# Moving the weight-cast copies out of the first attention chunk, six per weight load instead of four, and loading the output projection's weights earlier

## The chip, the cores and the metric

One Trainium2 chip, all 8 cores, one launch. Every core runs the same program on its own part of the data, and no core waits for another. The metric is the device time of the slowest core in microseconds (us).

## The reference

```python
x  = hidden_states                      # (4, 2048, 2048) f32
xn = layernorm(x)
q, k, v = xn @ Wq.T + bq, xn @ Wk.T + bk, xn @ Wv.T + bv   # 16, 8, 8 heads of 128
q, k = rope(q), rope(k)                 # k, v then repeated to 16 heads
feat = lambda t: [sin(p), cos(p)] / sqrt(128),  p = (t / |t|) @ R.T
s  = ((feat(q) . feat(k_j)) weighted sum over the heads j of v_j, per token) @ Wo.T + bo
h  = silu(xn @ W1.T) * (xn @ W3.T)      # 8192 wide
g  = silu(fwht(h) @ W2.T)               # fwht: Hadamard transform of length 8192
out = x + s * g
```

The mixing of heads is per token, so nothing is carried along the sequence.

## The kernel before

A pair of cores shares one of the four batches. Each core does the attention part for all 2048 tokens of its batch and 8 of the 16 query heads, and the feed-forward part (FFN) for its own 1024 tokens.

**Attention.** `for ac in range(n_ac)` runs over 4 chunks of 512 tokens (here chunk 0 to chunk 3), each of 4 tiles of 128 tokens (`ts`). A chunk has these steps:

- `emit_ln_chunk`: SyncE loads a tile of x (`XBa`, `XBb`, L200); ScalarE takes the sum of squares by a Square whose elementwise output nobody reads (L211, into a scratch region that the argument `sqf` names); VectorE makes the mean and the normalized tile `XNa`/`XNb` (L242); TensorE transposes it, and ScalarE copies it to `XNT` (L265). The loads of the first two tiles of a chunk are issued as soon as the buffers are free, which is in the chunk before.
- QKV: six jobs (`ji` 0 to 5: two for q, two for k, two for v), each with one weight load of 2 MB of bf16, cast from 4 MB of f32 as it is loaded, alternately into `WA` and `WB`. `emit_p1g` issues the load on GpSimd's DMA queue (L335), once the job that used the buffer last is done. `emit_p1t` is the job's matmuls (L355, L359); it then has the load of job `ji + 2` issued. The last job stands apart in `emit_p1_tail` (L414, L417). For a chunk after the first, its jobs 0 and 1 have their loads issued when jobs 4 and 5 of the chunk before are done.
- features: rope on VectorE, transposes, the product with `RT16`, then for each tile `p2wrap`, `p2sin`, `p3a` (64 small products on VectorE, L721), and the mixing of values, half of it on VectorE (`p3m`, L591 to L603) and half on GpSimd (`p3p`, L739 to L749). TensorE transposes the result (L615), ScalarE copies it to `MIXT` (L625).

The chunks overlap: behind tile `ts` of the feature loop of chunk c stands job `ts + 1` of chunk c + 1, and the LayerNorm and job 0 of chunk c + 1 stand ahead of that loop. All engines take their instructions in the order of the program. On GpSimd the loads of weights and `p3p` are in one stream: `p3p` of tile 0 stands behind the load of job 3, and that waits for job 1.

**The casts.** The FFN reads its weights W1, W3 and W2 as bf16 from device memory. `emit_casts` makes these copies: 96 DMAs from device memory to device memory (L323), each reading 2 MB of f32 and writing 1 MB of bf16. They stand in `cast_list` in the order W1, W3, W2. `emit_p1g` issues 4 of them behind each of the 24 weight loads of the attention part, on the same queue:

```python
    def emit_casts(g, kmax=4):
        for _ in range(kmax):
            if cast_ptr[0] >= len(cast_list):
                return
```

Nothing in the attention part reads them; the first FFN load waits for them (`dwe`, L945).

**Output projection.** `attn_done` collects the last work of VectorE, ScalarE and GpSimd; then four blocks of 512 columns (`dc`), each with a weight load from `WOT` (`p4g`, L799) and 8 x 16 matmuls (L816). The first two loads are issued behind the last `p3p`.

**FFN.** Two passes of 512 tokens (`oc2`): LayerNorm as above from `XOWN`; W1 and W3 (L970, L975), the Hadamard transform over device memory (`S1`, `S2`), W2 (L1179), silu (L1194), the product with s and the sum with x on VectorE (L1211, L1215), and the output (L1227). The buffers of a pass's LayerNorm lie where those of the pass before for x and the output lay (`XRES`, `OUTB`), so the load at L200 waits for the output's DMAs (`out_slot_tok`).

Of the kernel before, what the change touches and what calls it, by code (L numbers as in the profile page):

```python
# [17 lines left out]
DM = 2048  # L18
# [42 lines left out]
def build_program(t_own=TOWN, t_batch=TBATCH, t_chunk=512, debug=False):  # L61
# [126 lines left out]
    def emit_ln_chunk(blk, xsrc, row0, pT, pT_free, sqf, extra_war=()):  # L188
        XBa, XBb = bufs["XBa"], bufs["XBb"]
        XNa, XNb = bufs["XNa"], bufs["XNb"]  # L190
        for ts in range(NT):
# [5 lines left out]
            def p0ld(sp, ts=ts, xb=xb, dxs=dxs):  # L197
                tk.wait(sp, "sp", *out_slot_tok, tk.tok("dbg"), *extra_war)
                tk.wait(sp, "sp", xb_cons_dv[ts % 2], xb_cons_ac[ts % 2])
                tk.inc(sp.dma_start(  # L200
                    xb[:, :],
                    bass.AP(xsrc, (row0 + ts * 128) * DM, [[DM, 128], [1, DM]]),
                ), dxs, 16)
                st["x"] = tk.tok(dxs)
# [3 lines left out]
            def p0a(a, ts=ts, xsl=xsl):  # L208
                tk.wait(a, ACT, st["x"], cst_tok, *extra_war)
                tk.wait(a, ACT, xb_cons_dv[ts % 2], xb_cons_ac[ts % 2])  # L210
                st["sq"] = tk.inc(a.activation(sqf(ts), xsl, AF.Square,  # L211
                                               accum_out=rcol(ts, C_SUMSQ)), "ac")
# [78 lines left out]
    SQF_OFF = 6144  # L291
    MIX_OFF = 10240
    sqf_attn = lambda ts: bass.AP(SBf, SQF_OFF + (ts % 2) * DM, [[SBW, 128], [1, DM]])
# [13 lines left out]

    jobs = ([(WQTS, BQs, QB, oc) for oc in range(2)]
# [8 lines left out]
    def emit_casts(g, kmax=4):  # L317
# [10 lines left out]
    def emit_p1g(blk, c, ji):  # L328
# [4 lines left out]
        def p1g(g, buf=buf, sem=sem, wd=wd, oc=oc, ji=ji, evt=evt):  # L333
# [6 lines left out]
            emit_casts(g)  # L340
# [96 lines left out]
    for ac in range(n_ac):  # L437
        arow0 = ac * t_chunk

        if ac == 0:  # L440
            with BLK() as blk:
                emit_ln_chunk(blk, XBAT, 0, [pT[0]], pT_free, sqf_attn)
                emit_p1_main(blk, 0, full=True)
                emit_p1_tail(blk, 0, None)
# [127 lines left out]
        if ac + 1 < n_ac:  # L572
            with BLK() as blk:
                emit_ln_chunk(blk, XBAT, (ac + 1) * t_chunk, [pT[0]], pT_free, sqf_attn)
                emit_p1_main(blk, ac + 1)
# [54 lines left out]
        with BLK() as blk:  # L630
            for ts in range(NT):
# [97 lines left out]
                if nxt is not None:  # L729
                    emit_p1t(blk, nxt, ts + 1)  # L730

# [58 lines left out]
    with BLK() as blk:  # L790
        evt = {}
        bank_tok = {}
        for dc in range(4):
            buf, sem = (WA, "dwa") if dc % 2 == 0 else (WB, "dwb")

            def p4g(g, dc=dc, buf=buf, sem=sem):
                tk.wait(g, "pl", tk.tok("dbg"))
                tk.wait(g, "pl", wcons[sem])
                tk.inc(g.dma_start(  # L799
                    bass.AP(buf, 0, [[8192, 128], [1, 8192]]),  # L800
                    bass.AP(WOT, dc * 128 * 8192, [[8192, 128], [1, 8192]]),
                ), sem, 16)
                evt[("w", dc)] = tk.tok(sem)
            blk.gpsimd(p4g)

            for r in range(NSUB):
                def p4t(t, dc=dc, r=r, buf=buf):
                    tk.wait(t, "pe", evt[("w", dc)], bank_tok.get(r % 4), *attn_done)
# [10 lines left out]
                    evt[("mm", dc, r)] = tk.inc(last, "pe")  # L819
                blk.tensor(p4t)  # L820

                if r % 2 == 0:
                    def p4v(v, dc=dc, r=r):
                        tk.wait(v, DVE, evt[("mm", dc, r)])
# [5 lines left out]
                else:  # L830
                    def p4a(a, dc=dc, r=r):
                        tk.wait(a, ACT, evt[("mm", dc, r)])
# [24 lines left out]
    sqf_ffn = lambda ts: bass.AP(GT8, (ts % 2) * DM, [[NT * 2 * 512, 128], [1, DM]])  # L857
# [3 lines left out]
    ffn_prev = []  # L861
    s1_free = [()]
    s2_free = [()]

    for oc2 in range(n_oc):
# [11 lines left out]
        with BLK() as blk:  # L877
            emit_ln_chunk(blk, XOWN, orow0, pT, pT_free, sqf_ffn,
                          extra_war=tuple(p4b_done) + tuple(ffn_prev))
# [55 lines left out]
        with BLK() as blk:  # L935
            upt = {}
            for gb in range(32):
# [3 lines left out]
                def p5g(g, gb=gb, b1=b1, s1_=s1_, b3=b3, s3_=s3_):  # L941
                    tk.wait(g, "pl", tk.tok("dbg"), *out_slot_tok, *p4b_done)
# [16 lines left out]
                for al in range(2):  # L959
# [33 lines left out]
                    def p5v(v, a_=a_, pl_=pl_):  # L993
                        tk.wait(v, DVE, upt[("silu", a_)], p4b_done[0])
# [239 lines left out]
        ffn_prev = [tk.tok("dv"), tk.tok("ac")]  # L1234
        p67.close()
# [86 lines left out]
```

How the kernel before makes its waits and increments, by code:

```python
    def inc(self, instr, name, n=1):  # L43
        self.cnt[name] += n
        instr.then_inc(self.h[name], n)
        return (name, self.cnt[name])
# [4 lines left out]
    def wait(self, eng, ek, *toks):  # L51
        for t in toks:
            if t is None:
                continue
            name, v = t
            if v > 0 and self.waited.get((ek, name), 0) < v:
                eng.wait_ge(self.h[name], v)
                self.waited[(ek, name)] = v
```

## Time and profile before

| what | us |
|---|---|
| three runs, median (lowest, highest) | 3519.12 (3518.92, 3695.49) |
| the profiled execution, its own time | 3519.18 |
| its span on the slowest core, core 5 | 3517.6 |
| spans of the 8 cores | 3496.7 to 3517.6 |
| start to the end of chunk 3's last QKV job, core 5 | 1277 |
| start to the first matmul of the output projection, core 5 | 1503.2 |

The profiled execution stands for the runs: its time is the median's, within 0.1 us. Its time exceeds its span by 1.6 us, which is what lies before the first and after the last instruction. All times inside the program are us from the span's start on core 5. "PE" is TensorE, "DVE" VectorE, "ACT" ScalarE, "POOL" GpSimd, "SP" SyncE. In a timeline row the first number is the start, the second how long, and the bracket the idle time before it and what ended it.

### The profile page before, as it was taken

What the parts mean: (1) busy time and instruction counts of PE and PEld (TensorE: products, weight loads), DVE (VectorE), ACT (ScalarE), POOL (GpSimd) and SP (SyncE); (2) the same over time, 40 slices, a digit from 0 to 9 for tenths busy, and PEclk for the clock granted to TensorE, in tenths of its full rate; (3) what the DMA queues carried; (4) which work ended last, traced back from release to release, by engine and by line L of the source; (5) the groups of instructions that cost most, each with busy time, mean ns of one, the idle gap of its engine ahead of it and who ended that gap; (6) DMA issues with size and microseconds to landing.
All of it is one profiled execution on the core that took longest, in us unless ns stands there. A gap on an engine that the chain in (4) does not pass through costs nothing.

```text
span 3517.6 us, 27856 instructions; the slowest of 8 cores (3496.7 to 3517.6 us)
## 1 busy us (share of the span) xinstructions
PE 2093.1 (60%) x9600; PEld 951.6 (27%) x9600; DVE 1134.7 (32%) x3436; ACT 758.8 (22%) x852; POOL 473.4 (13%) x587
## 2 busy tenths in 40 slices
PE   0624144344416430095799994468919999932987
PEld 0202111211212120053344442033414444410433
DVE  1030368457816869801111111501031111123011
ACT  2203511531152140014322221000042222200000
POOL 1000045014402524400000000000000000000000
PEclk9967576566657665597899997589959999965999
DMA  8999999999998950041344447555333444467353
GB/s 132 148 127 126 147 134 126 127 154 126 123 142 107 125 84 0 12 84 48 136 175 156 168 156 176 121 194 186 137 118 140 168 173 156 168 131 202 137 176 131
DMA packets 134091, 472.74 MB, mean 134 GB/s; under 512 B 11584, under 2 KB 93504, under 8 KB 97600
## 3 DMA queue, kind: packets, MB, share of 16 engines
q0 software_dynamic: 41152, 361.90, 51.3%
q1 hardware_dynamic: 50432, 75.50, 7.6%
q10 hardware_dynamic: 42368, 33.56, 3.9%
q8 instruction: 78, 1.28, 0.2%
q14 instruction: 61, 0.50, 0.1%
HBM read 589.55 MB, written 142.61 MB: 208 GB/s over the span
## 4 chain that ended last, share of the span: by engine, by line
PE 53%; DMA 14%; DVE 10%; POOL 8%; ACT 8%; another core or an unknown queue 3%; issue 3%; ACTq 1%; DVEq 0%; POOLq 0%; SPq 0%
PE p L970 13%; PE p L975 13%; PE p L1179 12%; PE p L359 7%; DMA XBb<-XBAT 5%; DMA U<-S 4%; PE p L816 3%; POOL PSCR L739 3%; DVE TMP L721 3%; DVE U L1066 3%; POOL PSCR L741 2%; PE p L417 2%; DMA S<-U 1%; POOL PSCR L744 1%
## 5 line engine op out<-in xcount | busy, mean ns | idle before, releaser
L996 DVE TENSOR_TENSOR U<-GT,p 128x512 bf16<-128x512 bf16 x128 | 88.1, 688 | 754.1 <-ACT GT L988 754.1
L1179 PE MATMUL p<-WA,U 128*128 128x512 bf16 x1024 | 235.0, 389 | 134.5 <-DMA U<-S 118.4
L988 ACT ACT_TABLE_LOAD x128 | 164.2, 1283 | 682.2 <-PE p L975 676.9
L615 PE MATMUL pT<-IDENTs,SBf 128*128 128x128 bf16 x128 | 16.2, 306 | 450.2 <-POOL SBf L749 306.2
L721 DVE SCALAR_TENSOR_TENSOR TMP<-QP,KP 128x128 bf16<-128x128 bf16 x1024 | 228.0, 286 | 121.0 <-POOL SBf L749 93.6
L970 PE MATMUL p<-XNT,WA 128*128 128x512 bf16 x1024 | 236.0, 384 | 13.1 <-DMA W3A<-W3Bd 13.1
L1179 PE MATMUL p<-WB,U 128*128 128x512 bf16 x1024 | 227.9, 381 | 7.2 <-DMA WB<-W2Bd 7.2
L975 PE MATMUL p<-XNT,W3A 128*128 128x512 bf16 x1024 | 231.5, 379 | 0.0
L975 PE MATMUL p<-XNT,W3B 128*128 128x512 bf16 x1024 | 231.5, 379 | 0.0
L970 PE MATMUL p<-XNT,WB 128*128 128x512 bf16 x1024 | 231.5, 379 | 0.0
L1211 DVE TENSOR_TENSOR TMPR<-SBf,GT 128x512 bf16<-128x512 bf16 x32 | 13.6, 425 | 587.5 <-ACT GT L1194 584.3
L359 PE MATMUL p<-WA,XNT 128*128 128x512 bf16 x768 | 197.2, 415 | 0.0
L1194 ACT ACT_TABLE_LOAD x4 | 5.1, 1283 | 788.3 <-PE p L1179 788.3
L1179 PEld LDWEIGHTS p<-WA,U 128*128 128x128 bf16 x1024 | 101.7, 100 | 264.0 <-issue 150.7
L739 POOL TENSOR_TENSOR PSCR<-VB,ROWS 128x1024 bf16<-128x1024 bf16 x64 | 128.3, 2005 | 204.0 <-DVE TMP L721 197.0
L1057 PE MATMUL p<-U,BLK64b 128*128 128x512 bf16 x128 | 72.8, 581 | 126.6 <-DMA U<-S 100.9
L970 PEld LDWEIGHTS p<-XNT,WA 128*128 128x128 bf16 x1024 | 101.1, 99 | 137.5 <-issue 19.8
L615 PEld LDWEIGHTS pT<-IDENTs,SBf 128*128 128x128 bf16 x128 | 12.4, 137 | 456.6 <-issue 456.6
L1179 PEld LDWEIGHTS p<-WB,U 128*128 128x128 bf16 x1024 | 100.3, 98 | 130.1 <-issue 11.3
L970 PEld LDWEIGHTS p<-XNT,WB 128*128 128x128 bf16 x1024 | 100.3, 98 | 120.8
L975 PEld LDWEIGHTS p<-XNT,W3A 128*128 128x128 bf16 x1024 | 100.2, 98 | 120.8
L975 PEld LDWEIGHTS p<-XNT,W3B 128*128 128x128 bf16 x1024 | 100.2, 98 | 120.8
(160 smaller groups left out, 2687.1 us busy)
## 6 DMA issues: line engine op xcount, KB each, us to landing
W1Bd<-W1T POOLq DMA_DIRECT2D x32, 1024.0 KB, 97.4
W3Bd<-W3T POOLq DMA_DIRECT2D x32, 1024.0 KB, 82.4
W2Bd<-W2T POOLq DMA_DIRECT2D x32, 1024.0 KB, 86.5
WA<-W1Bd POOLq DMA_DIRECT2D x32, 1024.0 KB, 5.3
W3A<-W3Bd POOLq DMA_DIRECT2D x32, 1024.0 KB, 8.0
WB<-W1Bd POOLq DMA_DIRECT2D x32, 1024.0 KB, 5.2
W3B<-W3Bd POOLq DMA_DIRECT2D x32, 1024.0 KB, 7.5
WA<-W2Bd POOLq DMA_DIRECT2D x32, 1024.0 KB, 5.1
```

The lines of the kernel that those rows point to most:

```text
L359: last = t.matmul(bank[:, :], XNT[:, k * t_chunk + ts * 128: k * t_chunk + (ts + 1) * 128], buf[:, k * 512:(k + 1) * 512], start=False, st ...
L417: last = t.matmul(bank[:, :], XNT[:, k * t_chunk + ts * 128: k * t_chunk + (ts + 1) * 128], WB[:, k * 512:(k + 1) * 512], start=False, sto ...
L721: ins = v.scalar_tensor_tensor(ATMP[:, j * 128:(j + 1) * 128], qsl, 1.0 / 64.0, ksl, op0=ALU.mult, op1=ALU.mult, accum_out=ROWS[:, 96 + h ...
L739: tk.inc(g.tensor_tensor(PSCR[:, :], vfull, abb, op=ALU.mult), "po")
L816: last = t.matmul(bank[:, :], lhsT, buf[:, m * 512:(m + 1) * 512], start=False, stop=(m == 15))
L970: last = t.matmul(pu[:, :t_chunk], b1[:, k * 256 + al * 128: k * 256 + (al + 1) * 128], XNT[:, k * t_chunk:(k + 1) * t_chunk], start=(k == ...
L975: last = t.matmul(pl_[:, :t_chunk], b3[:, k * 256 + al * 128: k * 256 + (al + 1) * 128], XNT[:, k * t_chunk:(k + 1) * t_chunk], start=(k = ...
L988: upt[("silu", a_)] = tk.inc(a.activation(GT[:, (a_ % 2) * 512:(a_ % 2) * 512 + t_chunk], pu[:, :t_chunk], AF.Silu), "ac")
L996: upt[("gate", a_)] = tk.inc(v.tensor_tensor(U[:, a_ * t_chunk:(a_ + 1) * t_chunk], GT[:, (a_ % 2) * 512:(a_ % 2) * 512 + t_chunk], pl_[:, ...
L1057: ins = t.matmul(bank[:, :], BLK64[:, :], U[:, ch * 512:(ch + 1) * 512], start=True, stop=True)
L1066: fw[("e64", ch)] = tk.inc(v.tensor_copy(U[:, ch * 512:(ch + 1) * 512], bank[:, :]), "dv")
L1179: last = t.matmul(bank[:, :], U[:, a_ * t_chunk + ts * 128: a_ * t_chunk + (ts + 1) * 128], buf[:, al * 1024 + dc * 512: al * 1024 + (dc + ...
```

## The change

It has four parts.

1. `emit_casts` issues up to 6 casts (`kmax=6`) and is not called for the loads of chunk 0. All 96 are issued behind 16 loads: those of chunk 1 and chunk 2 and of jobs 0 to 3 of chunk 3.
2. In the feature loop of chunk 3 the loads of the first two blocks of the output projection's weights are issued ahead of `p3p` of tiles 0 and 1 (`emit_p4g`). The other two are issued where they were.
3. The Square of `emit_ln_chunk` writes into `XNa`/`XNb` instead of a region of its own; `sqf` is gone.
4. Waits of the FFN are told apart: `extra_war` of the second pass is the last silu alone (`p5_war`) instead of the last work of VectorE and ScalarE and of the output projection; the load at L200 waits for `xres_slot_tok` besides `out_slot_tok`; `xnt_cons` is set behind the W1/W3 matmuls.

```diff
-    def emit_ln_chunk(blk, xsrc, row0, pT, pT_free, sqf, extra_war=()):
+    def emit_ln_chunk(blk, xsrc, row0, pT, pT_free, extra_war=()):
...
-                tk.wait(sp, "sp", *out_slot_tok, tk.tok("dbg"), *extra_war)
+                tk.wait(sp, "sp", tk.tok("dbg"), *extra_war)
+                tk.wait(sp, "sp", *out_slot_tok, *xres_slot_tok)
...
-                st["sq"] = tk.inc(a.activation(sqf(ts), xsl, AF.Square,
+                st["sq"] = tk.inc(a.activation(xn[:, :], xsl, AF.Square,
...
+    def emit_p4g(blk, dc):
+        buf, sem = (WA, "dwa") if dc % 2 == 0 else (WB, "dwb")
+
+        def p4g(g, dc=dc, buf=buf, sem=sem):
+            tk.wait(g, "pl", tk.tok("dbg"))
+            tk.wait(g, "pl", wcons[sem])
+            tk.inc(g.dma_start(
+                bass.AP(buf, 0, [[8192, 128], [1, 8192]]),
+                bass.AP(WOT, dc * 128 * 8192, [[8192, 128], [1, 8192]]),
+            ), sem, 16)
+            p4evt[("w", dc)] = tk.tok(sem)
+        blk.gpsimd(p4g)
...
-    def emit_casts(g, kmax=4):
+    def emit_casts(g, kmax=6):
...
-            emit_casts(g)
+            if c > 0:
+                emit_casts(g)
...
                 if nxt is not None:
                     emit_p1t(blk, nxt, ts + 1)
+                elif ts < 2:
+                    emit_p4g(blk, ts)
...
+            if dc >= 2:
+                emit_p4g(blk, dc)
...
-            emit_ln_chunk(blk, XOWN, orow0, pT, pT_free, sqf_ffn,
-                          extra_war=tuple(p4b_done) + tuple(ffn_prev))
+            emit_ln_chunk(blk, XOWN, orow0, pT, pT_free,
+                          extra_war=tuple(p5_war))
...
-                    tk.wait(g, "pl", tk.tok("dbg"), *out_slot_tok, *p4b_done)
+                    tk.wait(g, "pl", tk.tok("dbg"), *out_slot_tok, *xres_slot_tok)
...
-                                pT_free[0], pT_free[1], p4b_done[1], p4b_done[2])
+                                pT_free[0], pT_free[1], *p5_war)
...
-                        tk.wait(v, DVE, upt[("silu", a_)], p4b_done[0])
+                        tk.wait(v, DVE, upt[("silu", a_)])
...
+        xnt_cons[0] = tk.tok("pe")
...
+        p5_war = [dn[("silu", 1)]]
```

The start of GpSimd's stream, behind the constants, before the change: the weight loads of jobs 0 to 3 of chunk 0 (`WA`, `WB`), each with its casts (`W1Bd`).

```order
L341 UNCONDITIONAL_BRANCH
L335 DMA WA<-WQTS 128x8192
L323 DMA W1Bd<-W1T 32x16384 x4
L341 UNCONDITIONAL_BRANCH
L335 DMA WB<-WQTS 128x8192
L323 DMA W1Bd<-W1T 32x16384 x4
L341 UNCONDITIONAL_BRANCH
L335 DMA WA<-WKT 128x8192
L323 DMA W1Bd<-W1T 32x16384 x4
```

The same stream now, from the load of job 3 of chunk 0 to that of job 1 of chunk 1.

```order
L356 UNCONDITIONAL_BRANCH
L349 DMA WB<-WKT 128x8192
L356 UNCONDITIONAL_BRANCH
L349 DMA WA<-WVT 128x8192
L356 UNCONDITIONAL_BRANCH
L349 DMA WB<-WVT 128x8192
L356 UNCONDITIONAL_BRANCH
L349 DMA WA<-WQTS 128x8192
L337 DMA W1Bd<-W1T 32x16384 x6
L356 UNCONDITIONAL_BRANCH
L349 DMA WB<-WQTS 128x8192
L337 DMA W1Bd<-W1T 32x16384 x6
```

Chunk 0 has its six loads bare, and from chunk 1 on each load has six casts behind it.

GpSimd's stream at the end of the attention part, before the change: the last value mixing of tile 3 of chunk 3, and then the first two loads of the output projection's weights.

```order
L739 TENSOR_TENSOR PSCR<-VB,ROWS 128x1024
L741 TENSOR_TENSOR PSCR<-PSCR 128x512
L744 TENSOR_TENSOR PSCR<-PSCR 128x256
L749 TENSOR_TENSOR SBf<-PSCR 128x128
L804 UNCONDITIONAL_BRANCH
L799 DMA WA<-WOT 128x8192
L804 UNCONDITIONAL_BRANCH
L799 DMA WB<-WOT 128x8192
```

The same loads now: the second of them, between the value mixing of tile 0 and that of tile 1 of chunk 3.

```order
L756 TENSOR_TENSOR PSCR<-VB,ROWS 128x1024
L758 TENSOR_TENSOR PSCR<-PSCR 128x512
L761 TENSOR_TENSOR PSCR<-PSCR 128x256
L766 TENSOR_TENSOR SBf<-PSCR 128x128
L320 UNCONDITIONAL_BRANCH
L315 DMA WB<-WOT 128x8192
L768 UNCONDITIONAL_BRANCH
L756 TENSOR_TENSOR PSCR<-VB,ROWS 128x1024
```

SyncE's load at the start of the second FFN pass, with the semaphores that it waits for, before (first) and now (second); `do0` to `do3` count the output's DMAs.

```order
L200 DMA XBaf<-XOWN 128x2048 [waits do0,do1,do2,do3,ac]
L201 DMA XBaf<-XOWN 128x2048 [waits ac,do0,do1,do2,do3]
```

The same five semaphores are waited for, in another order. On TensorE, VectorE and ScalarE no instruction moves.

## Rows read from the trace of the kernel before

**Rows 1.** The page: DMA share in 40 slices of 88 us, the casting queue, HBM.

```profile
DMA  8999999999998950041344447555333444467353
...
q0 software_dynamic: 41152, 361.90, 51.3%
...
HBM read 589.55 MB, written 142.61 MB: 208 GB/s over the span
```

**Rows 2.** Windows: stretch, its length, busy us (instructions) by engine, clock, DMA.

```profile
core 5: us, PE busy (x) PEld busy (x) DVE busy (x) ACT busy (x) POOL busy (x), PEclk, DMA share, GB/s
460.00:1082.00 622.00, 237.02 (x1199) 110.95 (x1197) 372.17 (x1401) 187.72 (x222) 179.64 (x183) 0.66 0.99 131
1082.00:1290.00 208.00, 100.42 (x462) 43.05 (x461) 158.39 (x588) 38.95 (x54) 85.90 (x84) 0.72 0.94 122
1308.00:1490.00 182.00, 4.05 (x32) 3.10 (x32) 160.25 (x656) 18.82 (x25) 76.00 (x66) 0.50 0.01 2
```

**Rows 3.** Timeline of TensorE: first matmul of a job that follows a wait.

```profile
158.25 0.58 PE L355 MATMUL p<-BKs,ONESs 1*128 1x512 bf16 x1 [14.39 <-DMA WA<-WKT]
...
308.22 0.58 PE L414 MATMUL p<-BVs,ONESs 1*128 1x512 bf16 x1 [31.20 <-DMA WB<-WVT]
...
624.18 0.58 PE L414 MATMUL p<-BVs,ONESs 1*128 1x512 bf16 x1 [8.39 <-DMA WB<-WVT]
...
1258.93 0.58 PE L414 MATMUL p<-BVs,ONESs 1*128 1x512 bf16 x1 [5.32 <-ACT VB L404]
```

**Rows 4.** Timeline of GpSimd: loads of jobs 3, 4, 5 of chunk 3.

```profile
1102.20 0.56 POOL L335 DMA_DIRECT2D WB<-WKT  x1 [12.99 <-PE p L359]
...
1145.08 0.60 POOL L335 DMA_DIRECT2D WA<-WVT  x1 [21.65 <-PE p L359]
...
1189.99 0.60 POOL L335 DMA_DIRECT2D WB<-WVT  x1 [21.12 <-PE p L359]
```

**Rows 5.** Line L335: issue to landing, loads issued at 21.88, 1102.20, 1145.08, 1189.99.

```profile
DMA to landing us min/median/max: 23.9/23.9/23.9
...
DMA to landing us min/median/max: 54.7/54.7/54.7
...
DMA to landing us min/median/max: 61.9/61.9/61.9
...
DMA to landing us min/median/max: 68.7/68.7/68.7
```

**Rows 6.** Line L323: issue to landing, the four casts issued from 1102.8, then from 1190.6.

```profile
DMA to landing us min/median/max: 63.0/76.3/87.2
...
DMA to landing us min/median/max: 77.7/88.1/94.7
```

**Rows 7.** Timeline of VectorE, LayerNorm of chunk 0, last three tiles.

```profile
45.76 2.29 DVE L218 TENSOR_REDUCE ROWS<-XBb 128x1 f32<-128x2048 f32 x1 [10.49 <-DMA XBb<-XBAT]
...
76.42 2.29 DVE L218 TENSOR_REDUCE ROWS<-XBa 128x1 f32<-128x2048 f32 x1 [23.51 <-DMA XBa<-XBAT]
...
96.26 2.29 DVE L218 TENSOR_REDUCE ROWS<-XBb 128x1 f32<-128x2048 f32 x1 [12.62 <-DMA XBb<-XBAT]
```

**Rows 8.** Timeline, chunk 0: TensorE's job 0 starts, GpSimd issues behind jobs 0 and 1.

```profile
111.12 0.58 PE L355 MATMUL p<-BQs,ONESs 1*128 1x512 bf16 x1 [2.53 <-ACT XNT L265]
...
128.91 0.57 POOL L335 DMA_DIRECT2D WA<-WKT  x1 [101.94 <-PE p L359]
...
144.41 0.57 POOL L335 DMA_DIRECT2D WB<-WKT  x1 [12.97 <-PE p L359]
```

**Rows 9.** Timeline, end of the attention part: GpSimd, ScalarE, TensorE.

```profile
1486.82 0.60 POOL L799 DMA_DIRECT2D WA<-WOT  x1
...
1489.38 1.01 ACT L625 COPY MIXT<-pT 128x1024 bf16<-128x1024 bf16 x1
...
1503.17 0.58 PE L810 MATMUL p<-BOs,ONESs 1*128 1x512 bf16 x1 [15.17 <-DMA WA<-WOT]
```

**Rows 10.** Timeline of SyncE, first load of the second FFN pass.

```profile
2573.95 0.34 SPq L200 DMA_DIRECT2D XBaf<-XOWN  x1
```

More of the change, by code:

```diff
@@ L206, in emit_ln_chunk, with p0a @@
             xsl = xb[:, :]
-            def p0a(a, ts=ts, xsl=xsl):
+            def p0a(a, ts=ts, xsl=xsl, xn=xn):
                 tk.wait(a, ACT, st["x"], cst_tok, *extra_war)
                 tk.wait(a, ACT, xb_cons_dv[ts % 2], xb_cons_ac[ts % 2])
-                st["sq"] = tk.inc(a.activation(sqf(ts), xsl, AF.Square,
+                st["sq"] = tk.inc(a.activation(xn[:, :], xsl, AF.Square,
                                                accum_out=rcol(ts, C_SUMSQ)), "ac")
@@ L290, in build_program @@
     P0Q_OFF, P0K_OFF = 2048, 4096
-    SQF_OFF = 6144
     MIX_OFF = 10240
-    sqf_attn = lambda ts: bass.AP(SBf, SQF_OFF + (ts % 2) * DM, [[SBW, 128], [1, DM]])
     pctx = contextlib.ExitStack()
@@ L306, in build_program @@
     pool_prev = [None]
+    p4evt = {}
+    def emit_p4g(blk, dc):
[9 more added lines that the diff above has]
+        blk.gpsimd(p4g)
     jobs = ([(WQTS, BQs, QB, oc) for oc in range(2)]
@@ L441, in build_program @@
             with BLK() as blk:
-                emit_ln_chunk(blk, XBAT, 0, [pT[0]], pT_free, sqf_attn)
+                emit_ln_chunk(blk, XBAT, 0, [pT[0]], pT_free)
                 emit_p1_main(blk, 0, full=True)
@@ L573, in build_program @@
             with BLK() as blk:
-                emit_ln_chunk(blk, XBAT, (ac + 1) * t_chunk, [pT[0]], pT_free, sqf_attn)
+                emit_ln_chunk(blk, XBAT, (ac + 1) * t_chunk, [pT[0]], pT_free)
                 emit_p1_main(blk, ac + 1)
@@ L790, in build_program @@
     with BLK() as blk:
-        evt = {}
         bank_tok = {}
@@ L794, in build_program @@
             buf, sem = (WA, "dwa") if dc % 2 == 0 else (WB, "dwb")
[L796 to L804, printed above, removed]
+            if dc >= 2:
+                emit_p4g(blk, dc)
             for r in range(NSUB):
                 def p4t(t, dc=dc, r=r, buf=buf):
-                    tk.wait(t, "pe", evt[("w", dc)], bank_tok.get(r % 4), *attn_done)
+                    tk.wait(t, "pe", p4evt[("w", dc)], bank_tok.get(r % 4), *attn_done)
                     bank = P[r % 4]
@@ L818, in p4t @@
                                         start=False, stop=(m == 15))
-                    evt[("mm", dc, r)] = tk.inc(last, "pe")
+                    p4evt[("mm", dc, r)] = tk.inc(last, "pe")
                 blk.tensor(p4t)
@@ L823, in p4v @@
                     def p4v(v, dc=dc, r=r):
-                        tk.wait(v, DVE, evt[("mm", dc, r)])
+                        tk.wait(v, DVE, p4evt[("mm", dc, r)])
                         tk.wait(v, DVE, tk.tok("dv"))
@@ L831, in p4a @@
                     def p4a(a, dc=dc, r=r):
-                        tk.wait(a, ACT, evt[("mm", dc, r)])
+                        tk.wait(a, ACT, p4evt[("mm", dc, r)])
                         tk.wait(a, ACT, tk.tok("ac"))
@@ L856, in build_program @@
     GT8 = fsb0("GT8", [128, NT * 2 * 512], BF16)
-    sqf_ffn = lambda ts: bass.AP(GT8, (ts % 2) * DM, [[NT * 2 * 512, 128], [1, DM]])
     TMPR = fsb0("TMPR", [128, 512], BF16)
@@ L861, in build_program @@
     ffn_prev = []
+    p5_war = list(p4b_done)
     s1_free = [()]
```

## The prediction

> **What bounds the kernel now.** I read the page first. Its line of DMA shares stands at 8 or 9 tenths in the first 14 slices of 88 us, to about 1230 us, and then falls to almost nothing [rows 1]: the attention part runs against a saturated DMA until all casts are made, and has it idle afterwards. The windows say the same with a sum: 0.99 from 460 to 1082 us, 0.94 from there to 1290, 0.01 from 1308 to 1490 [rows 2]. In none of these windows is an engine full; DVE with 372 of 622 us is the nearest.
>
> Then TensorE's timeline, for who waits for the weights. In chunk 0 every job from the third on starts after a wait of 14 to 32 us that a weight load ends (four such rows, the first and the last in [rows 3]; 110 us in all). In chunks 1 and 2 only the last job waits for its load, 8.4 us [rows 3]. Job 5 of chunk 3 starts at 1258.93; its load landed at 1189.99 + 68.7 = 1258.7 [rows 4, 5], together with ScalarE's copies that the row names [rows 3]. So chunk 0 is bound by the queue. In the later chunks the queue and the engines' own chain (value mixing on GpSimd, transposes, a job, next mixing) are nearly level.
>
> Last, the pace of the queue. Weight loads of jobs 3, 4 and 5 of chunk 3 land at 1102.20 + 54.7 = 1156.9, 1145.08 + 61.9 = 1207.0, and 1258.7 [rows 4, 5]. They wait in line behind one another's casts: **one weight load and four casts take 50.9 us**.
>
> **Part 1, the casts.** The number of casts stays 96; they move from 24 loads to 16. What this does depends on the price of one cast in a full queue. From below: the last of four casts issued from 1102.8 (half a us apiece, so the last at 1104.2) lands at 1104.2 + 87.2 = 1191.4, which is 34.5 us behind the load ahead of it, 8.6 each [rows 5, 6]. From above: a cast moves 3 MB (2 read, 1 written) and a weight load reads 4, so by bytes a cast is 3/16 of 50.9 = 9.5. I take 9.0, the middle, and 14.9 for the load. The far end is 6.2: the last four casts of all land 94.7 - 77.7 = 17 us apart although issued 1.5 us apart, (17 + 1.5) / 3 [rows 6]. These run when other cores have drained, so I keep it for a rival. Tiles of x (1 MB read) cost a quarter of a load, 3.7.
>
> *Chunk 0 gets faster.* The second tile arrives at 45.8 as before. The third and fourth now wait only for two bare weight loads and the tiles themselves: 2 x 14.9 + 4 x 3.7 = 45 us from 21.9, at 66 at the latest, at 60.7 if the LayerNorm is the limit (a tile takes 111.12 - 96.26 = 14.9 from its arrival [rows 7, 8]). I take 63, so job 0 starts at 63 + 29.8 = 93, before 111 [rows 8]. A job that starts after a wait takes 128.91 - 111.12 = 17.8, one without 15.5 [rows 8]. A load in an idle queue takes 1503.17 - 1486.82 = 16.4 [rows 9]. Job 0 ends at 110.8, job 2's load lands at 127.2, and then the jobs and the loads step at about 15.9: job 4 ends at 175. There job 5 starts, before at 308.2 [rows 3], and chunk 1's first load is issued.
>
> *Chunks 1 to 3 get slower.* From there the queue is the clock. Each cycle is one load and six casts, 50.9 + 2 x 9.0 = 68.9, against some 45 that the chain of mixing and job needs (1189.99 - 1145.08 = 44.9 from one issue to the next [rows 4]). The first load lands at 191. The load of job 3 of chunk 3 is 15 cycles and 10 tiles of x later: 1033.5 + 37. The same sum made for the kernel before (first load lands at 21.88 + 23.9 = 45.8 [rows 5], 21 cycles of 50.9, 14 tiles) gives 1166.5 where 1156.9 was measured, 9.6 too late in 21 cycles; I take off 7 for 15 cycles. So 191 + 1033.5 + 37 - 7 = 1254.5. Job 4's load has the last six casts ahead of it: 1323.4. Job 4 takes 17.8, transposes, copy and ScalarE's turn to the next evictions about 6 (the first two are 3.6 at the end of the attention part [rows 9], from 1486.8 to 1490.4; the rest is my estimate), and job 5 starts at 1347.2, before at 1258.9. **+88.3.** Job 5's own load has no casts ahead and lands 14.9 behind job 4's, in time. What follows job 5, features and mixing of chunk 3 without any DMA [rows 2], is unchanged.
>
> Why a step that frees 133 us in chunk 0 ends 88 us late: before, the queue had hardly a gap ahead of the load of job 3 of chunk 3, and 84 casts there; now it has 90, and between 22 and 175 us it holds only six loads and six tiles, about 112 us of work in 153. Six casts more are 54, the gap about 40. It lasts because the end of the attention part hangs on the last QKV loads, and these now stand behind every cast; before, four casts stood behind the last load and cost nobody.
>
> The casts' issue on GpSimd is 0.5 us apiece; two more per load hide in the 24 us by which the chain is now ahead of the queue.
>
> **Part 2, the output projection's loads.** Now TensorE waits for the load from when `MIXT` is copied, 1490.4, to 1503.17 [rows 9]. With the load long landed the first matmul comes about 0.2 us behind the copy: **-12.6**. Their place ahead of `p3p` costs GpSimd two issues of 0.6 us; both buffers are free there, and the DMA is idle then. The third load has the 31 us of the second block to hide in, as now.
>
> **Part 3, Square into `XNa`/`XNb`:** same engine, shape and type, and its readers' waits stand already. Nothing. **Part 4, the FFN's waits:** the load that opens the second pass starts at 2573.95 [rows 10] and waits for the same five semaphores, so nothing there can start earlier; `xres_slot_tok` and `xnt_cons` name work that is long done. Nothing. The FFN's first load waits for the casts, which end near 1310, ahead of the output projection.
>
> **Sum.** 3519.2 (the profiled execution, level with the median of 3519.1) + 88.3 - 12.6 = **3595 us**.
>
> **Rivals.**
> - *A. The marginal cast is cheap (not slower).* If in a full queue a further cast costs the 6.2 of the last batch [rows 6], a cycle is 63.3, the load of job 4 comes 16 x 5.6 = 90 us earlier, job 5 starts where it does now and only the -12.6 stays: 3506. The change breaks even at 88.3 - 12.6 = 75.7 less, 75.7 / 32 = 2.4 less per cast, at 6.6 us. For it: that batch. Against it: the cycle keeps to 50.1 and 51.7 while all cores stream, and now they stream together to the end. Here the Trainium skill speaks for the forecast ("HBM Reference", section "Specifications (TRN2)"): a core alone gets about 425 GB/s, each of two streaming cores of a pair about 358, an estimated 7.4 and 8.8 us per cast, so the cheap last batch is a core whose partner is done. The trace's 330 GB/s (16.8 MB in 50.9 us) lies below both.
> - *B. The queue is not the bound.* Then chunk 0's gain stays: job 5 of chunk 0 starts at 175 instead of 308.2, the later chunks keep the engines' pace and lose their waits of 8.4, as much again and 5.3 [rows 3]: -155 - 12.6, 3352. It needs a cycle under 45. Against it stands the 50.9 with only four casts. A page of the Trainium skill would bring it about: "DMA: Bandwidth & Descriptors", section "Anatomy of one DMA", has a transfer cost 2.0 us and its bytes at 436 GB/s; with the fixed part hidden in a full queue that makes an estimated 4.8 us per cast and 9.6 per load, 38 per cycle of six. By that rule the cycle of four would be 29, and the trace's 50.9 speaks against it for copies within device memory on all cores.
> - *C. The deeper queue holds up GpSimd.* Before, the deepest point is about 127 us of work in line; now about 185 at the loads issued at a chunk's end (two batches of six and two loads and what is left of a third). If the issue blocks when the line is full, `p3p` behind it starts late. It can cost at most about one mixing, some 20 us: 3615. For it: nothing seen; issues took 0.56 to 0.60 us at every depth [rows 4, 8].
>
> **Chances.** Forecast 0.76, with its own range 3570 to 3618 (cast at 8.6 to 9.5 moves it by -13 and +16; the arrival of tiles in chunk 0 by 5); A or a price on the way to it 0.10; B 0.04; C 0.10. About 2% is what a measurement tells here from no change, and 2% is 3589.5: the forecast's case falls below it in about a third. So slower by over 2% 0.57, within 2% 0.38, faster 0.05. Range for 8 in 10: 3550 to 3622.
>
> **What would show it.** Right: job 0 of chunk 0 at about 93 us, chunk 1's first load issued near 175, weight loads landing 69 us apart in chunks 2 and 3 with TensorE waiting for them at nearly every job, job 5 of chunk 3 near 1347, no wait for the output projection's load, and the FFN as long as before. Wrong: landings 63 apart or closer (A), no waits for loads in chunks 1 to 3 (B), GpSimd idle or long issues at the casts (C), or a gap in the DMA share after 200 us.

## The result, and the profile after

| | before | changed |
|---|---|---|
| time, median of 10 runs each (lowest) | 3525.25 us (3518.92) | 3618.62 us (3610.24) |
| ratio, 95% interval | | 1.0278 (1.0240 to 1.0316) |
| span of the slowest core in the profiled execution | 3517.6 (core 5) | 3614.0 (core 4) |
| span of core 5 | 3517.6 | 3603.4 |

The change makes the kernel 2.8% slower. Whatever the kernel, in some executions the cores of one die or of both take longer at a lower granted clock, and every ratio here is of the other executions alone. The page of the changed kernel: DMA share and clock in 40 slices, now of 90 us, the casting queue, HBM.

```profile
PEclk9957655655656566569699999569968999965999
DMA  6599999999999981102244444664523444467453
...
q0 software_dynamic: 41152, 361.90, 50.0%
...
HBM read 589.55 MB, written 142.61 MB: 203 GB/s over the span
```

The bytes are those of [rows 1]. The first two slices have the DMA at 6 and 5 tenths where they stood at 8 and 9, and the full stretch ends one slice later (a slice is itself 2 us longer). The windows of the changed kernel, core 4, with the columns of [rows 2]:

```profile
22.00:175.00 153.00, 92.01 (x421) 39.85 (x421) 44.53 (x68) 55.60 (x61) 5.54 (x12) 1.00 0.61 125
187.00:1000.00 813.00, 248.51 (x1250) 115.47 (x1248) 360.16 (x1458) 191.35 (x226) 186.39 (x212) 0.63 1.00 128
1000.00:1254.00 254.00, 74.57 (x427) 38.09 (x424) 97.20 (x507) 80.56 (x92) 44.47 (x54) 0.61 1.00 126
1400.00:1587.00 187.00, 4.04 (x40) 3.19 (x40) 160.19 (x657) 23.01 (x31) 75.45 (x65) 0.51 0.06 12
```

Chunk 0 uses 0.61 of the DMA, then it is full to 1254 us and beyond, and the features of chunk 3 have it idle as before, so the work that was missing in chunk 0 is done where somebody waits. In the full stretch DVE is busy 360 of 813 us, and in that of [rows 2] 372 of 622.

TensorE's first matmuls behind a wait, core 4, which answer to [rows 3] (bracket: idle before, and what ended it):

```profile
123.78 0.37 PE L370 MATMUL p<-BKs,ONESs 1*128 1x512 bf16 x1 [0.57 <-DMA WA<-WKT]
...
413.02 0.58 PE L370 MATMUL p<-BKs,ONESs 1*128 1x512 bf16 x1 [18.98 <-DMA WB<-WKT]
...
483.50 0.58 PE L370 MATMUL p<-BVs,ONESs 1*128 1x512 bf16 x1 [27.96 <-DMA WA<-WVT]
...
552.50 0.58 PE L429 MATMUL p<-BVs,ONESs 1*128 1x512 bf16 x1 [51.10 <-DMA WB<-WVT]
...
775.64 0.58 PE L370 MATMUL p<-BKs,ONESs 1*128 1x512 bf16 x1 [32.83 <-DMA WA<-WKT]
...
985.90 0.58 PE L429 MATMUL p<-BVs,ONESs 1*128 1x512 bf16 x1 [51.36 <-DMA WB<-WVT]
...
1336.92 0.58 PE L370 MATMUL p<-BVs,ONESs 1*128 1x512 bf16 x1 [26.64 <-DMA WA<-WVT]
...
1359.20 0.58 PE L429 MATMUL p<-BVs,ONESs 1*128 1x512 bf16 x1 [4.43 <-ACT VB L419]
```

In chunk 0 the waits of 14 to 32 us have shrunk to less than one. From chunk 1 on, ten of the 18 jobs on this core start after a wait of 19 to 51 us that their weight load ends: jobs 3 to 5 of chunk 1, jobs 2 to 5 of chunk 2 and jobs 2 to 4 of chunk 3. Jobs 0 and 1 of a chunk wait 1.3 us at most for their loads. The landings follow from GpSimd's issues (loads of jobs 3, 4, 5 of chunk 2 and job 0 of chunk 3, core 4) and the time from issue to landing of the same four:

```profile
719.42 0.56 POOL L349 DMA_DIRECT2D WB<-WKT  x1 [13.32 <-PE p L374]
...
794.34 0.60 POOL L349 DMA_DIRECT2D WA<-WVT  x1 [52.69 <-PE p L374]
...
863.67 0.60 POOL L349 DMA_DIRECT2D WB<-WVT  x1 [46.77 <-PE p L374]
...
934.66 0.60 POOL L349 DMA_DIRECT2D WA<-WQTS  x1 [9.99 <-PE pT L630]
```

```profile
DMA to landing us min/median/max: 126.3/126.3/126.3
...
DMA to landing us min/median/max: 121.7/121.7/121.7
...
DMA to landing us min/median/max: 122.0/122.0/122.0
...
DMA to landing us min/median/max: 121.0/121.0/121.0
```

They land at 845.7, 916.0, 985.7 and 1055.7, **70.0 us apart**, where [rows 4, 5] have 50.9. From issue to landing these loads take 121 to 126 us; those of [rows 5] in a full queue took 55 to 69. At the end of the attention part, ScalarE and TensorE (which answer to [rows 9]):

```profile
1589.73 1.01 ACT L640 COPY MIXT<-pT 128x1024 bf16<-128x1024 bf16 x1
...
1590.89 0.58 PE L818 MATMUL p<-BOs,ONESs 1*128 1x512 bf16 x1 [2.53 <-ACT MIXT L640]
```

The wait for the output projection's load is gone. On core 5, whose trace of before the prediction used, the marks of the two kernels are these (start of the last QKV job of each chunk; start of the output projection):

| core 5 | job 5 of chunk 0 | chunk 1 | chunk 2 | chunk 3 | output projection | span |
|---|---|---|---|---|---|---|
| before | 308.2 | 624.2 | 942.3 | 1258.9 | 1503.2 | 3517.6 |
| changed | 167.5 | 543.1 | 976.1 | 1352.5 | 1584.2 | 3603.4 |
| difference | -141 | -81 | +34 | +94 | +81 | +86 |

The 141 us won in chunk 0 are given back at 60, 115 and 60 us a chunk.

### The profile page after: what moved, and what is told of

Its sections match the earlier page's. It is cut to its first block, busy times and chain, and to the rows that moved or that the text cites. A ratio compares the mean times of both kernels' runs of the same rounds, so it can differ in the third digit from the quotient of the medians.

```text
span 3614.0 us, 27859 instructions; the slowest of 8 cores (3588.5 to 3614.0 us)
## 1 busy us (share of the span) xinstructions
PE 2084.6 (58%) x9600; PEld 950.0 (26%) x9600; DVE 1091.1 (30%) x3436; ACT 759.1 (21%) x852; POOL 461.5 (13%) x587
## 4 chain that ended last, share of the span: by engine, by line
PE 53%; DMA 12%; DVE 10%; another core or an unknown queue 9%; ACT 8%; POOL 5%; issue 3%; ACTq 0%; DVEq 0%; POOLq 0%; SPq 0%
PE p L978 12%; PE p L983 12%; PE p L1189 12%; PE p L374 8%; DMA U<-S 4%; PE p L824 3%; DVE U L1076 2%; DMA XBb<-XBAT 2%; POOL PSCR L756 2%; DVE TMP L736 2%; DMA XBa<-XBAT 2%; PE p L432 2%; DMA S<-U 1%; POOL PSCR L758 1%
## 5 line engine op out<-in xcount | busy, mean ns | idle before, releaser
L630 PE MATMUL pT<-IDENTs,SBf 128*128 128x128 bf16 x128 | 15.0, 291 | 384.5 <-POOL SBf L766 240.5
L1076 DVE CAST U<-p 128x512 bf16<-128x512 f32 x128 | 88.5, 692 | 112.6 <-PE p L1067 99.3
```

Of the source, the lines that this page charges most:

```text
L1076: fw[("e64", ch)] = tk.inc(v.tensor_copy(U[:, ch * 512:(ch + 1) * 512], bank[:, :]), "dv")
```

## The experiments

The theory: the attention part runs at the pace of one queue, and what counts in it is which of the loads that somebody waits for stand behind which casts. Rivals were that the early loads of the output projection or the new waits cost something, that the depth of the queue or the number of casts per load counts wherever they stand, and that the queue's gap in chunk 0 is itself the loss. The experiments ran on other chips than the table above. The kernel before has medians from 3537 to 3541 us there, and each ratio is to the kernel before on the same chip.

**e1: part 1 undone, the rest of the change kept.**

```diff
-    def emit_casts(g, kmax=6):
+    def emit_casts(g, kmax=4):
...
-            if c > 0:
-                emit_casts(g)
+            emit_casts(g)
```

> Part 1 undone: four casts behind each of the 24 loads again; the output projection's early loads, the Square's new target and the FFN's waits stay. Queue theory (the whole slowdown is that the last QKV loads stand behind every cast): 12 to 13 us faster than the kernel before, about 3512, with the first matmul of the output projection near 1491 us. Rival (the early loads or the new waits cost something themselves): level with the kernel before or slower.

Measured: 3525.31 us, ratio 0.9957 (0.9926 to 0.9987). By the medians that is 12 us less than the 3537.38 of before, by the ratio 15. The output projection starts at 1498.2 on core 5, 231.3 behind job 5 of chunk 3, where the kernel before has 1503.17 - 1258.93 = 244.2: 13 us for the early loads. Without part 1 nothing is left of the slowdown.

**e2: the kernel before with part 1 alone.**

```diff
-    def emit_casts(g, kmax=4):
+    def emit_casts(g, kmax=6):
...
-            emit_casts(g)
+            if c > 0:
+                emit_casts(g)
```

> The kernel before with part 1 alone: six casts behind each load from chunk 1 on, none in chunk 0; the output projection's loads where they were. Queue theory: as the changed kernel plus the 12 to 13 us of the late load, a first matmul of the output projection near 1603 us and a time near 3630. Rival (the early loads of the output projection take DMA time from the last QKV loads): level with the changed kernel, near 3617.

Measured: 3633.78 us, ratio 1.0251 (1.0187 to 1.0315), so part 1 alone makes the slowdown. The output projection starts at 1604.6 on core 5 and 1615.7 on core 4, 20 and 25 later than in the changed kernel. From job 5 of chunk 3 to there it is 240.5 and 244.9 us, in the changed kernel 231.7 on both: 9 and 13 us are the late load, and the rest lies ahead of job 5 (1364.1 against 1352.5 on core 5). The ratios of the two kernels overlap, so the time does not show the 12 to 13 us. The rival fails on the trace: with the early loads job 5 starts no later than without them, and the changed kernel issues the first of them at 1348.2 on core 5, when the last QKV load has landed (1341.1).

**e3: parts 3 and 4 alone** (e1 with the output projection's loads back in their old place).

```diff
-                elif ts < 2:
-                    emit_p4g(blk, ts)
...
-            if dc >= 2:
-                emit_p4g(blk, dc)
+            emit_p4g(blk, dc)
```

> Parts 3 and 4 alone (the Square writes into the normalized tile's buffer, the FFN's waits told apart); casts and output projection's loads as before. Queue theory: no difference, within 4 us of the kernel before, and the FFN as long as before. Rival (the 9 us by which the changed kernel's execution grew behind the start of the output projection come from parts 3 and 4): about 9 us slower.

Measured: 3535.49 us, ratio 0.9982 (0.9952 to 1.0013), no difference. From the start of the output projection to the end it takes 2015.2 us on core 5 and 2020.1 on core 4, before 2014.4 and 2010.8, in the changed kernel 2019.3 and 2023.2. The scatter is larger than any difference here: over the eight cores of one execution this stretch runs from 2006 to 2020 us in e3. Its mean over the cores is 2014.2 to 2015.6 in the four kernels with parts 3 and 4 (changed, e1, e3, e4) and 2011.5 and 2010.9 in the two without (before, e2), so some 3 us of cost are not ruled out.

**e4: the 24 casts of chunk 3's loads issued behind its last QKV load**, six ahead of each value mixing; chunks 1 and 2 keep six per load.

```diff
-            if c > 0:
-                emit_casts(g)
+            emit_casts(g, (0, 6, 6, 0)[c])
...
-                elif ts < 2:
-                    emit_p4g(blk, ts)
+                else:
+                    if ts < 2:
+                        emit_p4g(blk, ts)
+                    blk.gpsimd(lambda g: emit_casts(g, 6))
```

> The changed kernel, but the 24 casts of chunk 3's loads are issued behind its last QKV load, six ahead of each value mixing of chunk 3 on GpSimd. Chunks 1 and 2 keep six casts a load. Queue theory: chunk 2 ends near 1003 us as in the changed kernel, chunk 3 then runs at the engines' own pace, its job 5 starts near 1275 and the time is near 3525. Rival (what costs is six casts a load in all chunks, or the depth of the queue, wherever the last casts stand): over 3580. If late casts hold up the features, the mixing of chunk 3 takes over 215 us from job 5 to the output projection.

Measured: 3539.59 us, ratio 0.9995 (0.9966 to 1.0023). It makes the same 96 casts and has the same gap in chunk 0 and the same six per load in chunks 1 and 2, and is level with the kernel before. Against e1, which shares the early loads and ran on the same chip, it is still 14 us slower. Job 5 of chunk 2 starts at 986.6 on core 5 (changed kernel: 976.1), job 5 of chunk 3 then 292 us later instead of 376, at 1278.9; the forecast was near 1275. The two rows of TensorE, core 5:

```profile
1278.88 0.58 PE L428 MATMUL p<-BVs,ONESs 1*128 1x512 bf16 x1 [4.43 <-ACT VB L418]
...
1510.18 0.58 PE L819 MATMUL p<-BOs,ONESs 1*128 1x512 bf16 x1 [2.53 <-ACT MIXT L639]
```

So the rival (six per load cost wherever the last casts stand) fails for the time as a whole. Chunks 1 and 2 are not free of cost, though: they take 379 and 438 us, where the kernel before takes 316 and 318, and it is the gain of chunk 0 and the shorter chunk 3 (292 for 317) that pay for them. The features of chunk 3, from there to the output projection, take 231.3 us with the casts beside them. My expectation named 215 us as the mark for a held-up mixing; that mark was wrong, since the same stretch is 231.3 in e1 too, without any cast beside it but the last few. The time came 15 us above the 3525 that I had named, mostly since this chip has 3537 where the other had 3525.

**e7: eight casts per load**, so all 96 behind the 12 loads of chunks 1 and 2. It measures the price of a cast, the time by which a further cast in a full queue puts off what stands behind it.

```diff
-    def emit_casts(g, kmax=6):
+    def emit_casts(g, kmax=8):
```

> The changed kernel with eight casts behind each load: all 96 stand behind the 12 loads of chunks 1 and 2. It measures the price of a further cast: the cycle of landings is 50.9 + 4 times the price. Forecast's price 9.0: 87 us; 9.2, as the changed kernel's landings suggest: 88; rival A's 6.2: 76. Time near 3735 by queue theory, since chunk 2's last jobs come later still and chunk 3 can only start behind them.

Measured: 3911.03 to 4036.81 us in three runs, of which none can be compared with the other kernels. In the profiled one (3911.03) cores 4 to 7 have spans of 3745.0 to 3759.6 us, and the forecast was near 3735; the landings are read on core 5, where the span is 3757.8. GpSimd's loads of jobs 3, 4, 5 of chunk 1, and their times from issue to landing:

```profile
326.21 0.56 POOL L349 DMA_DIRECT2D WB<-WKT  x1 [10.93 <-PE p L374]
...
392.80 0.60 POOL L349 DMA_DIRECT2D WA<-WVT  x1 [43.41 <-PE p L374]
...
482.08 0.60 POOL L349 DMA_DIRECT2D WB<-WVT  x1 [66.05 <-PE p L374]
```

```profile
DMA to landing us min/median/max: 137.4/137.4/137.4
...
DMA to landing us min/median/max: 161.2/161.2/161.2
...
DMA to landing us min/median/max: 161.4/161.4/161.4
```

Landings at 463.6, 554.0 and 643.5: 90 us a cycle, and I had expected 87 to 88. With the other runs this makes a line: 3 casts 41.7 us (e6 below), 4 casts 50.9 (before) and 51.8 (e5), 6 casts 70.2 (changed, core 5), 8 casts 90. From 3 to 8 a cast costs (90 - 41.7) / 5 = **9.7 us** (between neighbouring points of the line 9.2 to 10.1), and the load itself 41.7 - 3 x 9.7 = 12.6. The ratio of the two is about 3 to 4, as their bytes (3 MB against 4). Rival A's 6.2 is out. The issues of these loads still take 0.56 to 0.60 us with 161 us of work in line, so rival C has nothing for it.

**e8: six casts behind each of the first 16 loads**, chunk 0 included.

```diff
-            if c > 0:
-                emit_casts(g)
+            emit_casts(g)
```

> Six casts behind each of the first 16 loads, chunk 0 included; loads of job 4 of chunk 2 and later are bare. The casts' number and the queue's total are as in the changed kernel, only the place differs, and there is no gap of the DMA in chunk 0. Queue theory: the loads up to job 5 of chunk 2 stand behind all 96 casts, and chunk 3's own work (some 290 us) comes behind that without any DMA to share: job 5 of chunk 3 near 1515, time near 3770. Rival (what the changed kernel lost is the queue's gap in chunk 0 and the total of the queue): faster than the changed kernel by the 40 us of the gap, near 3575.

Measured: 3797.10 us in its one run, beside 3538.39 for the kernel before. Job 5 of the four chunks starts at 407.8, 843.0, 1230.5 and 1522.1 on core 5. The DMA share is 1.00 from 22 to 1190 us. With no gap in the DMA and the same casts, the kernel is 259 us above the kernel before, and the changed one 93, although chunk 3 runs at its own pace (292 us). So the rival, which has it faster than the changed kernel, fails: filling the gap with casts only moves the waits into chunk 0, and the DMA of chunk 3 stays unused.

**e5: the version that the theory asks for.** No casts in chunk 0, four per load in chunks 1 to 3, 24 behind the last QKV load.

```diff
-            if c > 0:
-                emit_casts(g)
+            emit_casts(g, (0, 4, 4, 4)[c])
...
-                elif ts < 2:
-                    emit_p4g(blk, ts)
+                else:
+                    if ts < 2:
+                        emit_p4g(blk, ts)
+                    blk.gpsimd(lambda g: emit_casts(g, 6))
```

> Built from what the runs so far say: no casts in chunk 0, four behind each load of chunks 1 to 3 (72), the other 24 behind the last QKV load, in chunk 3's features, where the DMA was idle. Queue theory: chunk 0 keeps its gain of about 135 us, the later chunks need no more than before, job 5 of chunk 3 starts near 1125 us, and the time is near 3375, about 4% faster than before. Rival (the gain of chunk 0 is given back whatever stands behind, since the chunks are bound together by the engines' chain or by the number of casts): 3500 or more.

Measured: 3384.54 us, ratio **0.9573** (0.9548 to 0.9597); near 3375 was expected. Job 5 of chunk 3 starts at 1123.3 on core 5, as expected; the three chunks take 318, 319 and 315 us, in the kernel before 316, 318 and 317, and the gain of chunk 0 is kept (138 us at its job 5, 136 at that of chunk 3). A small wait is new: the third load of the output projection lands behind the last late casts, and TensorE waits 11 us for it. TensorE, core 5:

```profile
1123.31 0.58 PE L428 MATMUL p<-BVs,ONESs 1*128 1x512 bf16 x1 [7.67 <-DMA WB<-WVT]
...
1353.44 0.58 PE L819 MATMUL p<-BOs,ONESs 1*128 1x512 bf16 x1 [2.53 <-ACT MIXT L639]
...
1429.37 0.58 PE L819 MATMUL p<-BOs,ONESs 1*128 1x512 bf16 x1 [10.64 <-DMA WA<-WOT]
```

**e6: three per load, 42 behind** (`(0, 3, 3, 3)`, eleven ahead of each value mixing).

> As e5, with three casts behind each load of chunks 1 to 3 (54) and 42 behind the last QKV load. Queue theory: a cycle of one load and three casts is some 42 us, under the 45 of the chain, so the chunks now run at the chain's pace: up to 25 us faster than e5 in chunks 1 to 3, if the 42 late casts (near 380 us of queue) end before the first FFN load; they would end near 1480, that load comes near 1530. Rival (the queue still sets the pace at three casts): level with e5. If the late casts end too late, the first FFN pass starts with a wait and the time is above e5's.

Measured: 3484.71 us, ratio 0.9847 (0.9828 to 0.9867), 100 us above e5. The first half held: chunks 2 and 3 take 302 and 300 us on core 5 instead of 319 and 315, and the output projection starts at 1310.0. Then this row of TensorE, core 4:

```profile
1527.17 0.58 PE L819 MATMUL p<-BOs,ONESs 1*128 1x512 bf16 x1 [146.59 <-DMA WA<-WOT]
```

The third load of the output projection was issued at 1349.8 and stood behind 42 casts, which landed at 1514.5 at the last (expected near 1480). I had asked whether they would be done by the first FFN load and had overlooked the loads in between.

**e9: three per load, one in each of the last four loads of chunk 0, 24 at once behind the first load of the output projection, 14 behind its fourth.**

```diff
+            emit_casts(g, (int(ji > 1), 3, 3, 3)[c])
...
+                    if ts == 0:
+                        blk.gpsimd(lambda g: emit_casts(g, 24))
...
+            if dc == 3:
+                blk.gpsimd(lambda g: emit_casts(g, 96))
```

> Three casts behind each load of chunks 1 to 3, one behind each of the last four loads of chunk 0, 24 at once behind the first load of the output projection, 14 behind its fourth. In e6 the third load of the output projection stood behind the late casts and TensorE waited 147 us for it. Theory (what costs is only a load that somebody waits for standing behind casts): that wait is gone, the output projection starts near 1312 as in e6 and lasts its 130 us, time near 3350 on this chip, at best 3335, at worst 3365 if the 14 last casts hold up the first FFN load by 10 to 20 us. Rival (42 casts late are too much for the idle stretch however they stand): 3420 or more.

Its fastest run took 3415.72 us, the other three 3596 to 3731, so there is no interval. That is above the 3365 that I had set as the worst, and close to the rival's 3420. No load of the output projection is waited for any more, and it starts at 1318.6 on core 4. The time is lost behind it: the 14 last casts lie beside the LayerNorm of the first FFN pass, where SyncE issues the loads of tiles 2, 3 and 4 at 1449.2, 1495.1 and 1526.9, so 46 and 32 us apart, and the pass of [rows 10] has 12 and 13. The last cast lands at 1536.5 and the first FFN load is issued at 1559.3, 241 us behind the start of the output projection, where the kernel before has 183 on this core.

**e10: as e5, but the 24 late casts at once behind the first load of the output projection.**

```diff
-            if c > 0:
-                emit_casts(g)
+            emit_casts(g, (0, 4, 4, 4)[c])
...
                 elif ts < 2:
                     emit_p4g(blk, ts)
+                    if ts == 0:
+                        blk.gpsimd(lambda g: emit_casts(g, 24))
```

> As e5, but the 24 late casts are issued at once behind the first load of the output projection instead of six ahead of each value mixing. In e5 the third load of the output projection lands behind the last six casts and TensorE waits 11 us for it. Theory: the queue is empty near 1330 and that wait goes, 11 us less than e5, about 3373. Rival (24 casts in line hold up the second load, or the features): level with e5 or slower.

Measured: 3398.00 us, ratio 0.9625 (0.9586 to 0.9665), no better than e5. The reason is in TensorE's row at the second block, core 4:

```profile
1412.52 0.58 PE L819 MATMUL p<-BOs,ONESs 1*128 1x512 bf16 x1 [26.97 <-DMA WB<-WOT]
```

Now it is the second load that stands behind all 24, and they end at 1400.7, not near 1330: I had counted them from the wrong end. They follow the last QKV load, its own casts, which land at 1155.6, and the first load of the output projection, which lands at 1171.4, so 24 x 9.7 end close to 1400. Counted alone, 24 casts in 1400.7 - 1171.4 = 229.3 us are 9.6 each.

**e11 and e12: both first loads ahead of the 24, and e5 again on the same chip.**

```diff
-                elif ts < 2:
-                    emit_p4g(blk, ts)
+                elif ts == 0:
+                    emit_p4g(blk, 0)
+                    emit_p4g(blk, 1)
+                    blk.gpsimd(lambda g: emit_casts(g, 24))
```

> As e10 (four casts behind each load of chunks 1 to 3, 24 late ones at once), but the first two loads of the output projection both stand ahead of the 24. In e10 the second stood behind them and TensorE waited 27 us for it. Theory: the casts end near 1400 us, the second load has landed long before, the third lands when it is wanted (near 1414): no wait for any load of the output projection, 11 us faster than e5. Rival (the queue's work still reaches into the output projection): level with e5.

> e5 once more, on the same chip as e11, for the comparison: 0.957 of the kernel before, as before.

Measured: e11 3379.79 us, ratio 0.9552 (0.9512 to 0.9592); e12 3381.34 us, ratio 0.9552 (0.9505 to 0.9598). e11 still waits 8.1 us for the third load on core 4, where its theory had no wait and 11 us less than e5. The two are level, as the rival had it, and both are 4.5% faster than the kernel before and, by the two ratios, 7% faster than the changed one. Of the versions tried, these are the best.

## Why the prediction was right or wrong

The direction and the mechanism held, and the time lies in the range, 3 us below its upper end. The size fell short: +76 us were forecast, the profiled execution has +96 (3614.0 against 3517.6) and the medians +93. The step that failed is a term of the sum, the price of a further cast in a full queue.

- **The cycle, the term that was mis-sized.** I took a cast at 9.0, the middle between the 8.6 read from four landings and the 9.5 by bytes. It is 9.7 (e7, e6 and the changed kernel), and the cycle of six is 70.2 on core 5, not 68.9: 16 x 1.3 = 21 us too little. The landings of casts within one batch were a poor ruler. In [rows 4 to 6] the last cast of a batch lands early and the load behind it late: the four casts have 34.5 us and the load 15.6, where the line through e6 and e7 gives 38.8 and 12.6. The whole cycle divided by bytes was the right one of the two bounds. Why the landings divide it otherwise was not tried.
- **Chunk 0.** Job 0 was to start at 93 and started at 87.4 on core 5 (89.6 on core 4). The fourth tile of x landed at 60.3 on core 5, the earlier of my two cases, and job 0 started 27.1 behind it, not 29.8. Job 4 was to end at 175, and chunk 1's first load was issued at 168.1. Its landing was forecast at 191 and came at 181.9, 9 early.
- **The corrections.** The 7 us that I took off were not there, and a tile of x costs 2.5 us rather than 3.7 (1329.6 - 181.9 = 1147.7 for 16 cycles of 70.2 and ten tiles). Together +21 + 7 - 12, about +15 on a stretch forecast at 1132, less the 9 of the early start. The load of job 4 of chunk 3 landed at 1329.6 on core 5, forecast 1323.4, and job 5 started at 1352.5, forecast 1347.2. That these two came within 7 us is luck: two errors of 28 us together were nearly offset by two of 21 the other way.
- **The output projection's loads.** -12.6 forecast; 244.2 became 231.7 on core 5, 12.5. e1 has 13.
- **Parts 3 and 4.** Nothing forecast, and e3 finds nothing beyond the noise.
- **The rest of the shortfall.** The start of the output projection on core 5 came 5 us later than the sum. The core that ended last now is core 4, where it starts 7 us later still (1590.9 against 1584.2). Behind it core 4 takes 2023.2 us, 9 more than core 5 took before, and e3 shows scatter of that size. The sum followed core 5 alone. Its neighbour, core 4, was 13.5 us ahead at the output projection before (1489.6 against 1503.2) and is 6.7 behind now. In all four pairs of neighbours one core is 11 to 14 us ahead before and one is 7 to 9 ahead now, in three of the pairs the other one. The change is not needed for that: of the executions of e12, one kernel on one chip, one has the spans of cores 2 and 3 at 3358.2 and 3374.1 us and another at 3373.6 and 3355.0. The mean over the eight cores moved by 91 at the output projection, core 5 by 81.
- **Rivals.** A (a cheap marginal cast) fell to e7. The 6.2 of the last batch was the neighbour's doing, as I had supposed: before the change, in all four pairs, the casts of the later core that land wholly behind the last cast of its neighbour are 4.8 to 5.2 us apart, and those of the last batch that land before it 8.1 to 9.9. That is also less than the 7.4 us that I had estimated for a core alone from the 425 GB/s of the Trainium skill ("HBM Reference", section "Specifications (TRN2)"); here the measurement decides, though it rests on one or two landings a pair. Of the others, B (the queue is no bound) fell to the waits of 19 to 51 us in the changed kernel, C (issues blocked by a deep queue) to e7's 0.56 to 0.60 us per issue. The Trainium skill's rule of 2.0 us and 436 GB/s ("DMA: Bandwidth & Descriptors", section "Anatomy of one DMA"), by which the cycle of six would be an estimated 38 us, does not hold for these copies within device memory on all cores: the trace has 70.2. The 358 GB/s per core that the Trainium skill gives in "HBM Reference", section "Specifications (TRN2)", comes nearer, with an estimated 64 us for the cycle; the trace gives (18.9 + 4.2) MB in 70.2 us, 329 GB/s.

The explanation of why a gain of over 130 us ends as a loss stands. The load of job 3 of chunk 3 lands at 1260.9 on core 5, 104 us later than the 1156.9 of before: six casts more ahead of it are 58, and the other 46 are the gap in chunk 0, for which I had about 40. The experiments add what a cast costs in each place (time from job 5 of one chunk to job 5 of the next, core 5):

| casts behind each load of the chunk | time of the chunk, us | from |
|---|---|---|
| 0 | 292 | chunk 3 of e4 and of e8 |
| 3 | 302, 300 | chunks 2 and 3 of e6 |
| 4 | 315 to 319 | chunks 1 to 3 of the kernel before and of e5 |
| 6 | 433, 438 | chunk 2 of the changed kernel and of e4 |
| 8 | 553 | chunk 2 of e7 |

Up to four per load the engines' own pace hides the casts almost whole: 24 of them add some 25 us to a chunk, 1 each. Beyond four, each costs its full price: 12 more add 115 to 120 us, and 12 more again 114 to 120, 9.5 to 10 each. (Chunks 1 and 3 of the changed kernel take 376 us: the first starts with an empty queue, and the last has no casts behind its jobs 4 and 5.) In chunk 0 the jobs are short, and its 24 casts cost 141 us, 6 each. Behind the last QKV load lie some 200 us in which the kernel before computes and its DMA idles (its last cast lands at 1286.7, the next load is issued at 1486.8), and the 24 casts that e5 puts there cost an 11 us wait. So the number of casts ahead of the last QKV load does not set the time by itself: e4 has 72 there and e5 68, and e4 is 4% slower, since it puts six per load in two chunks and leaves the DMA of the third idle.

## What to carry to other kernels

Where one queue carries both urgent loads and work that only has to be done some time, compare in every stage the queue's cycle with the time that the engines need for it. Put the deferrable work where the engines are the slower side, up to the point where the two are level, and not beyond: here two casts more per load than that turned the 141 us won in chunk 0 into a loss of 2.8%, and 24 casts moved from chunk 0, where each was waited for, to the stretch behind the last QKV load were worth 4% (e5 against e1, by their ratios 0.9573 and 0.9957). Ask at every later load on the same queue whether the moved work now stands ahead of it (e6, e10: 147 and 27 us). If several cores share a memory, price the marginal transfer from whole cycles in the steady state, not from the landings within a batch. And do not read a difference of 10 us from one core of one execution: neighbouring cores change places from one execution to the next.

## What the runs showed of the hardware

- The price of a 2 MB to 1 MB casting copy within device memory, with all eight cores at it, is nearly constant from 3 to 8 copies per load (9.7 us each, 9.2 to 10.1 between neighbouring points; 9.6 in the row of 24 of e10), and the issues take no longer with 161 us of work in line.
- Once the neighbouring core's queue is empty, the landings of such copies come 4.8 to 5.2 us apart instead of 8.1 to 9.9 (last batch of the kernel before, all four pairs). So in the price of 9.7 us the neighbour has a large part.
- Late casts beside an engine stage that uses no DMA cost that stage nothing: 231.3 us with and without them (e4, e1). Beside the LayerNorm's loads of x, which come on another queue, they cost plenty: 46 and 32 us between loads that are else 12 to 13 apart (e9).
- Neighbouring cores do not run level in a saturated stretch (7 to 14 us apart at its end in the kernels before and changed), and which of them is ahead changes from one execution of a kernel to the next (e12, cores 2 and 3: 16 us one way, 19 the other). Why is open.
